# Two 16-head attentions: the divisor summed on VectorE before the weighting, the weights turned as one flat row, and more element-wise work on GpSimd

## The reference, cut to what matters

```python
# A: softmax with one more term in the divisor
attn = einsum('bhqd,bhkd->bhqk', qh * scale, kh)
e = exp(attn - max(attn))
attn = e / (1.0 + sum(e))
x = einsum('bhqk,bhkd->bhqd', attn, vh)      # then @ Wp.T + bp
# G: the same with a bias (16, 1024, 77) and a mask over the context rows
attn = where(mask, -inf, einsum('bhqd,bhkd->bhqk', q, k) * scale + bias)
probs = where(mask, 0.0, softmax(attn))
ctx = einsum('bhqk,bhkd->bhqd', probs / max(probs.sum(), 1e-6), v)   # then @ o_w.T + o_b
```

## Time and profile before

| | |
|---|---|
| median of 3 executions | 1403.33 us |
| the profiled execution | 1398.52 us, span 1396.5 us, mean granted clock 0.886 |
| busy, share of the span | PE 80%, PEld 60%, DVE 59%, ACT 42%, POOL 23% |
| layer A: first `shift` to last statistics | 24.2 to 166.1 us |
| layer G: first `shift` to last statistics | 955.4 to 1101.2 us |

### The profile page before, as it was taken

One profiled execution on the slowest core, in us unless ns is written; L12 is line 12 of the kernel. 1 busy time (PEld: TensorE's weight loads), 2 busy tenths in 40 slices (PEclk: granted clock), 3 DMA queues, 4 the chain that ended last, 5 costly groups with the idle time before them and its releaser, 6 DMA issues.

```text
span 1396.5 us, 22604 instructions
## 1 busy us (share of the span) xinstructions
PE 1121.6 (80%) x8519; PEld 844.9 (60%) x8519; DVE 819.8 (59%) x2107; ACT 580.9 (42%) x1448; POOL 314.9 (23%) x283
## 2 busy tenths in 40 slices
PE   4998799986989897957998899997888752996730
PEld 3666588884447545734666788884666731785530
DVE  5899722248558467972636764556888450552463
ACT  2665433342448535712415313225898440342210
POOL 0009134200435103420010000000000036435266
PEclk9899899995899899988999999997999655898775
DMA  9300054400000003000000720001221023444253
GB/s 316 129 2 2 19 160 131 125 1 0 1 0 2 1 1 121 2 12 12 1 23 2 202 90 1 0 1 37 74 74 38 24 84 105 135 136 115 92 152 118
DMA packets 59841, 88.74 MB, mean 64 GB/s; under 512 B 21315, under 2 KB 50749, under 8 KB 56925
## 3 DMA queue, kind: packets, MB, share of 16 engines
q1 hardware_dynamic: 52301, 67.05, 14.8%
q0 software_dynamic: 7440, 20.33, 5.3%
HBM read 60.60 MB, written 26.76 MB: 63 GB/s over the span
## 4 chain that ended last, share of the span: by engine, by line
PE 52%; DVE 19%; issue 11%; ACT 8%; POOL 4%; another core or an unknown queue 4%; DMA 1%; SPq 0%; POOLq 0%; DVEq 0%; ACTq 0%
PE ps L2571 5%; PE ps L1405 4%; PE ps L1939 4%; PE ps L800 4%; PE ps L813 4%; ACT work L487 2%; POOL pack_F L2830 2%; PE ps L2585 2%; PE ps L1950 2%; PE ps L380 2%; DVE dpack L1731 1%; PE ps L366 1%; DVE work L628 1%; ACT work L494 1%
## 5 line engine op out<-in xcount | busy, mean ns | idle before, releaser
L2822 POOL DMA_INDIRECT hall<-hall_rows,tile_idx x47 | 44.7, 950 | 381.0 <-DVE tile_idx L2728 328.2
L2571 PE MATMUL ps<-big,work 128*128 x316 | 89.2, 408 | 24.9 <-ACT work L2629 16.3
L1905 POOL TENSOR_TENSOR work<-work 128x512 f32<-128x512 f32 x64 | 65.1, 1039 | 143.6 <-DVE work L1753 143.6
L380 PE MATMUL ps<-work,hall 78*32 78x128 f32 (+1 forms) x2048 | 71.7, 282 | 17.4 <-ACT work L494 15.9
L2732 DVE TENSOR_TENSOR work<-work,ps 128x128 f32<-128x128 f32 x79 | 22.9, 290 | 106.4 <-ACT work L2633 51.0
L366 PE MATMUL ps<-pack_const,work 128*78 128x128 f32 (+1 forms) x512 | 73.8, 290 | 9.1 <-DVEq L593 9.1
L2571 PEld LDWEIGHTS ps<-big,work 128*128 128x128 f32 x316 | 58.1, 205 | 32.6 <-issue 27.4
L380 PEld LDWEIGHTS ps<-work,hall 78*32 78x32 f32 (+1 forms) x2048 | 53.9, 112 | 38.5 <-ACT work L494 33.2
L628 DVE RECIPROCAL work<-ps 128x128 f32<-128x128 f32 x64 | 60.8, 950 | 24.8 <-PE ps L380 24.8
L1855 ACT ACTIVATE work<-ps,work 128x256 f32<-128x256 f32 x128 | 58.9, 476 | 38.0 <-DVE work L1748 37.9
L487 ACT ACTIVATE work<-work 128x77 f32<-128x77 f32 x256 | 67.3, 347 | 14.3 <-DVE work L615 13.5
(11 more groups left out here) (515 smaller groups left out, 2644.9 us busy)
## 6 DMA issues: line engine op xcount, KB each, us to landing
expert_rows<-work SPq DMA_DIRECT2D x39, 256.0 KB
masked_bias<-hall SPq DMA_DIRECT2D x8, 1232.0 KB, 5.2
dpack<-masked_bias SPq DMA_DIRECT2D x8, 1232.0 KB, 6.2
hall<-in_fside SPq DMA_DIRECT2D x8, 616.0 KB, 7.4
dpack<-in_pack_D SPq DMA_DIRECT2D x1, 4115.0 KB, 15.7
big<-in_w SPq DMA_DIRECT2D x4, 1024.0 KB, 11.9
big<-in_pack_B SPq DMA_DIRECT2D x1, 2052.0 KB, 10.3
pack_F<-in_pack_F SPq DMA_DIRECT2D x1, 2052.0 KB, 22.4
```

What stands on the lines that cost most here:

```text
L380: mm = nc.tensor.matmul(ps[j * HB32:(j + 1) * HB32, 4, half:half + P], lhsT, A["pT"][0:SK[L], u % 2, h * P:(h + 1) * P], start=g == 0, sto ...
L2571: mm = nc.tensor.matmul(ps[:, GU_B[j % 2], 0:2 * INTER], MW["xT"][:, j % 2, c * P:(c + 1) * P], big[:, bass.ds(at + c * 2 * INTER, 2 * INT ...
```

## The change

Both attentions are rewritten on all four compute engines.

- The counting products are gone. DVE sums the exponentials of a unit (`tensor_reduce` of 128x624 in A, 128x616 in G), takes the reciprocal of 128x8 sums (`weigh_sum`), and POOL multiplies the exponentials by it, over 128x624 or 128x616 (`share`), before they are turned. `normalise` goes; ACT copies the 128x128 result out of PSUM instead (`take_o`).
- The weights of a unit are turned as one flat row of 8 x 78 or 8 x 77 columns, in five transposes of up to 128 columns; ACT copies 128x640. The values are laid out to match (`vflat`): with one-hot shifts of `vs` by 16 small matmuls at the start of a layer (`spread_values`), after which a unit needs 8 matmuls.
- In G the maximum is subtracted by POOL (`below_max`, 128x616), and ACT takes one exponential of 128x616.
- The projection's bias times its gate is added to x by POOL ahead of time (`gated_bias`, `add_bias`, 128x256), so `update` on DVE is two instructions.
- The loop runs over 16 groups `g` (one tile, two units) with three groups in flight.
- The rounding of B's weights moves from one run of twelve 128x2048 passes to pieces of 128x512, three and two passes each, placed on POOL between the shares of groups 9 to 16; the two all-reduces and scales stand behind the shares of group 6. `ffn_max_dve` is in groups 4 and 5.

Semaphores of other layers are renamed to make room; their order is the same.

```diff
+            def turn_p(k, xs):
+                pe.wait_ge(s("pn_ready"), k + 1 + done(L, "pn_ready"))
...
+                for r in range(NCHUNK):
+                    n = chunk_rows(L, r)
+                    mm = nc.tensor.transpose(ps[0:n, PT_BANK + r // 4, r % 4 * P:(r % 4 + 1) * P],
+                                             flat_weights(L, k)[:, r * P:r * P + n], ident)
...
+            def weigh_v(k):
+                m = k % (B * DC)
+                pe.wait_ge(s("pT_ready"), k + 1 + done(L, "pT_ready"))
...
+                for e in range(2):
+                    for j in range(HPG):
+                        r, g = VBLOCKS[2 * j + e]
+                        n = chunk_rows(L, r)
+                        mm = nc.tensor.matmul(ps[g * HB32:(g + 1) * HB32, 4, 0:P], KV["vflat"][0:n, 2 * j + e, m, :],
+                                              A["pT"][0:n, k % 2, r * P:(r + 1) * P], start=e == 0, stop=e == 1,
...
+            for g in range(NG16 + 2):            # PE
+                n, co = g // 2 + 1, g % 2
+                if n < HT:
+                    queries(n, co)
+                if g >= 2:
+                    weigh_v(2 * (g - 2) + 1)
+                if 1 <= g <= NG16:
+                    turn_p(2 * (g - 1), min(2 + g // 2, HT))
...
+                if g >= 2:
+                    project(g - 2)
+                if g % 2 and n + 1 < HT:
+                    turn_x(n + 1)
...
+                if 1 <= g <= NG16:
+                    weigh_v(2 * (g - 1))
+                if g + 1 < NG16:
+                    scores(g + 1)
...
+                if 1 <= g <= NG16:
+                    turn_p(2 * (g - 1) + 1, min(2 + (g + 1) // 2, HT))
...
                 else:
-                    for h in range(HPC):
-                        e = nc.scalar.activation(p[:, h, :], sub[:, h, :], ACT.Exp, bias=A["mx"][:, u % 2, h:h + 1])
-                    e.then_inc(s("p_ready"), 1)
+                    act.wait_ge(s("below_ready"), k + 1)
+                    nc.scalar.activation(p, sub, ACT.Exp).then_inc(s("p_ready"), 1)
...
+            for g in range(NG16 + 2):            # ACT
...
+                if 1 <= g <= NG16:
+                    exps(2 * (g - 1) + 1)
+                if n < HT:
+                    take_q(n, co)
...
+                if g >= 2:
+                    take_o(2 * (g - 2) + 1)
+                if 1 <= g <= NG16:
+                    take_pT(2 * (g - 1))
...
+                if g < NG16:
+                    exps(2 * g)
+                if 1 <= g <= NG16:
+                    take_o(2 * (g - 1))
...
+                if 1 <= g <= NG16:
+                    take_pT(2 * (g - 1) + 1)
...
+            gated_bias()                         # POOL
+            for g in range(NG16 + 1):
+                if g:
+                    share(2 * (g - 1))
+                if L == "A" and g >= QUANT_AT:
+                    ffn_round_pool(pool, g - QUANT_AT)
+                if L == "G" and g < NG16:
+                    below_max(2 * g)
+                if g:
+                    share(2 * (g - 1) + 1)
+                if L == "A" and g == QUANT_AT - 3:
+                    ffn_scale_pool(pool)
+                if L == "A" and g >= QUANT_AT:
+                    ffn_error_pool(pool, g - QUANT_AT)
+                if L == "G" and g < NG16:
+                    below_max(2 * g + 1)
+                if g < NG16:
+                    add_bias(g)
...
+            for g in range(NG16 + 2):            # DVE
+                if g < NG16:
+                    shift(g, 0)
...
+                if 1 <= g <= NG16:
+                    weigh_sum(2 * (g - 1) + 1)
...
+                if g < NG16:
+                    shift(g, 1)
...
+                if g >= 2:
+                    update(g - 2)
+                if g < NG16:
+                    weigh_sum(2 * g)
...
+        QUANT_AT = 9
+        QCOLS = 512
...
+            link(gp.tensor_scalar(q, w, inv, MAGIC, ALU.mult, ALU.add))
+            link(gp.tensor_scalar(q, q, -MAGIC, 127.0, ALU.add, ALU.min))
+            link(gp.tensor_scalar(q, q, -128.0, scale, ALU.max, ALU.mult))
...
+            chain_pool.link(gp.tensor_tensor(q, q, w, ALU.subtract))
+            gp.tensor_tensor(w, w, q, ALU.add).then_inc(sem("B_quantised"), 1)
```

More of the change, by code:

```diff
@@ L324, in turn_x @@
                 mm.then_inc(s("xT_ps"), 1)
-            def queries(n, parts=range(DC)):
-                if parts[0] == 0:
-                    pe.wait_ge(s("xT_ready"), nth(n, 1, 0) + done(L, "xT_ready"))
-                    if n >= 2:
-                        pe.wait_ge(s("x_new"), nth(n - 2, B, 0) + done(L, "x_new"))
-                for co in parts:
-                    for ci in range(DC):
-                        mm = nc.tensor.matmul(ps[:, Q_BANK, co * D:(co + 1) * D],
-                                              w["wq"][:, ci * D + co * P:ci * D + (co + 1) * P],
-                                              A["xnT"][:, ci, :], start=ci == 0, stop=ci == DC - 1)
-                if parts[-1] == DC - 1:
-                    mm.then_inc(s("q_ps"), 1)
@@ L349, in scores @@
+            def scores(g):
+                n, b = divmod(g, B)
+                if b == 0:
+                    pe.wait_ge(s("q_ready"), nth(n, 2, 1) + done(L, "q_ready"))
+                if g < 2:
+                    pe.wait_ge(s("kv_ready"), (2, 5)[g] + done(L, "kv_ready"))
+                if g:
+                    pe.wait_ge(s("sub_ready"), 2 * g + done(L, "sub_ready"))
+                for c in range(DC):
+                    at = c * HPT * SC
                     for j in range(S_TILES):
@@ L385, in project @@
-            def project(i, b, parts=range(DC)):
-                for c in parts:
-                    if c == 0:
-                        pe.wait_ge(s("on_ready"), nth(i, NU, 2 * b + 1) + done(L, "on_ready"))
-                        if b == 1:
-                            pe.wait_ge(s("q_ready"), min(i + 3, HT) + done(L, "q_ready"))
-                        if i or b:
-                            pe.wait_ge(s("x_new"), nth(i, B, b - 1) + done(L, "x_new"))
+                mm.then_inc(s("s_ps"), 1)
@@ L402, in heads16_pe @@
             turn_x(0)
[L403 removed]
+            queries(0, 0)
+            queries(0, 1)
             if L == "A":
                 values_ctx()
[L406 to L423 removed]
+            turn_x(1)
@@ L497, in heads16_act @@
[L497 to L517 removed]
+                    act.wait_ge(s("em_ready"), 2 * k + 1)
@@ new lines, in take_values, with take_spread @@
+                v = ve.tensor_tensor(vs, ps[0:SC, CTXV_BANK, :].rearrange("p (b n) -> p b n", b=B), bv, ALU.add)
+                if L == "G":
+                    for b in range(B):
+                        link(v)
+                        v = ve.tensor_scalar(vs[:, b, :], vs[:, b, :], keep[:, b:b + 1], None, ALU.mult)
+                v.then_inc(s("kv_ready"), 1)
+            def take_spread(part):
+                dve.wait_ge(s("kv_ps"), 3 + part + done(L, "kv_ps"))
+                half = KV["vflat"][:, part * NVB // 2:(part + 1) * NVB // 2].rearrange("p k m e -> p (k m e)")
+                ve.tensor_copy(half, ps[:, (CTXV_BANK, CTXK_BANK)[part], :]).then_inc(s("kv_ready"), 1)
@@ L638, in heads16_dve @@
             normed(1)
-            shift(0, 0)
+            take_values()
             spread_k(2)
             spread_k(3)
-            spread_v()
-            for n in range(HT):
-                shift(n, 1)
-                if L == "A" and n == 0:
+            for g in range(NG16 + 2):
+                if g < NG16:
+                    shift(g, 0)
+                if g == 0:
+                    take_spread(0)
+                    take_spread(1)
+                if 1 <= g <= NG16:
+                    weigh_sum(2 * (g - 1) + 1)
+                if L == "A" and g == 1:
+                    norm_std_dve(dve, "A1", REST)
+                    below(REST)
+                    dve.wait_ge(s("xT_ps"), 2 + done(L, "xT_ps"))
+                    normed(2)
+                    dve.wait_ge(sem("gates_ready"), 1)
+                if g < NG16:
+                    shift(g, 1)
+                if L == "A" and g == 0:
@@ L660, in heads16_dve @@
+                if L == "A" and g == QUANT_AT - 1:
                     ffn_inv_dve(dve)
[L661 to L674 removed]
```

425 lines of the change are left out of this document (200 added, 225 removed), and 12 rows, old and new, of the table TOTALS.

## The result

The changed kernel took 1407.0 us (median of 20 runs, 1398.5 to 1413.7), the kernel before 1396.1 us on the same chip (20 runs): ratio 1.0077, 95% interval 1.0059 to 1.0095. It is slower by 0.8%, where 1385 us and a gain were forecast. The profiled execution spans 1403.6 us, 7.1 more than that of before.

A forecast was written before the change was run, and what follows sets the result against it. DVE was taken as fullest in both layers, 6.3 us a group, with POOL pacing A's groups 9 to 15. G's -32.5 and A's +15 made -17.5 from 1403.3: 1386, stated as 1385 us, range 1366 to 1406.

The forecast's parts named there:

- three passes of 128x512: Rounding on POOL in layer A's groups 9 to 15: 0.65 us a pass, 1.9 us for the three.
- Groups 9 to 15: Layer A: POOL, not DVE, sets the pace at 7.5 us a group, 52.5 us for seven.
- The tail: End of layer A from group 16: share, rounding, share, then turn, copies, product, projection and update, 9 us.
- The all-reduces: Layer A, group 6: four POOL configuration changes, 2 x 6.7 + 2 x 6.9 = 27.2 us, giving 25.4 us of stop.
- the upper end: Change to an all-reduce costs between 0 and 6.7 us on POOL; 6.7 was taken.
- Rival 1: Layer A: changing to the all-reduce is free, stop 12.1 us instead of 25.4, kernel 1372 us; chance 0.17.
- Groups 2 to 8 with maxima and stop: Layer A: seven groups at 6.3 us (44.1), two maxima on DVE (4.6), all-reduce stop (25.4).
- -31.7 and -0.8: Layer G ends 31.7 us sooner; dropped zero-filling on DVE shortens layer F's end by 0.8 us.
- lower bound of 6.05: Steady group in A and G: DVE's summed work of 6.05 us with no wait at all.
- Rival 4, the clock: PE falls to half clock and stays, becoming the bound: 1438 us if everywhere; chance 0.11 for 1407 and above.
- Old order: Layer A: DVE's update no longer stopped by POOL's products, one operand now from PSUM; gain inside the sum.
- -32.5 against +15: Layer G gives back 32.5 us, layer A costs 15 us, together -17.5 us.

The follow-up runs named there:

- e1_same_kind: Changed kernel with its three rounding passes on POOL re-paired, arithmetic apart from min and max: 1381.9 us, 0.9881 of the kernel before.
- v3_again: Changed kernel with same-kind pairs, third pass writing the rounded weights, error products gone, maximum over partitions by TensorE and DVE: 1338.3 us, 0.9597 of the kernel before.
- e3_no_rounding: Changed kernel without all-reduces, rounding passes and error products, layer B's weights unrounded: 1341.0 us, 0.9584 of the kernel before.
- m1_prices: Changed kernel with a list of linked POOL instructions, 128x512 and 128x2048, ahead of layer A; one execution, read for durations only.
- b1_before_mixed: Kernel before with its rounding in the changed kernel's three mixed passes, each on 128x2048: 1405.4 us, 1.0064 of the kernel before.

## Why the prediction was wrong

The step that failed is the price of "three passes of 128x512 (0.18 fixed and a quarter of 1.9 each, 0.65: 1.9)" in the groups 9 to 15 of A. It took one price for all TENSOR_SCALAR passes from the earlier trace rows, where L745 pairs plus with times, while two of the three new passes pair plus with min and max with times. The kernel before had kept these apart, in four passes of 0.93 ns a column. Measured: 0.69 + 1.93 + 2.00 = 4.62. With that, the group took 10.66 us instead of 7.5, and POOL kept the bound that the forecast had rightly given it, at a much higher price; pairing the operations otherwise (e1_same_kind) gave back 21.6 us of A. That kernel takes 0.9881 of the kernel before, 16.6 us less on the scale of 1396, where 17.5 were forecast for the change: this one price decided the sign, and what else was off came near to cancelling out.

How the rest came out, by its own terms:
- **Groups 9 to 15**: 10.66 us instead of 7.5, 22 us for seven. Of the 3.16 us, 2.7 are the passes; the products (1.27 instead of 1.04) add 0.5, because their price was taken from L1905, which has one operand broadcast as a share has, while they read two whole tiles; the bias (0.72 instead of 0.46) adds 0.3; shares and gaps were cheaper. From group 9 to A's end the forecast had 61.5 us; there were 88.4 (DVE's first reduction of group 9 is at 117.88). This 26.9 is more than the whole miss of 24.6 (+7.1 by the profiled executions, against -17.5). The tail has 4.8 of it, 2.7 of them by the same passes in group 16.
- **The all-reduces**: the choice of the upper end was right. 26.12 us against 25.4, with 5.50, 7.38, 5.84 and 7.09 for what was taken as 6.7 and 6.9. Rival 1 falls. The rule of the Trainium skill (GPSIMD Engine Reference, section 2.1, Instruction dispatch), some 6 us for the first call to a freshly loaded kernel, agrees in size with all four gaps, 5.5 and 5.8 in one direction and 7.1 and 7.4 in the other, and the gap came at every change, not once.
- **Groups 2 to 8 with maxima and stop**: forecast 74.1, measured 74.5 (43.42 to 117.88). That is luck in part, since two errors cancel in it: the plain group took 5.73 us instead of 6.3 (DVE's shift 50.10, then 55.83), while the group with the stop took 0.65 more than its forecast and the one behind it 7.83 (110.05 to 117.88, with 1.1 us of other DVE work among it).
- **G**: -34.5 against -31.7 and -0.8. Its groups took 5.8 instead of 6.3, below even the lower bound of 6.05. The pass that reads PSUM (L685) took 0.75 and the sum (L701) 0.78 where 0.80 was taken, so that the durations of a group add up to 5.95; and many instructions are recorded as starting 0.08 to 0.09 us before the one ahead of them has ended, so that the steady group takes 5.71. Durations of rows, added up, are thus no lower bound of DVE's time. Its two ends cost 5 us more than written: groups 0 and 1 14.3 instead of 11.8, the tail 15.5 instead of 13.
- **Rival 4, the clock**: didn't happen, but its premise didn't come about either. PE's group was put at 4.5 us of 6.3, 71%; measured, the plain group of A from 50.10 to 55.83 has PE busy for 5.36 of 5.73 us, and the fourteen groups of G 5.28 of 5.82, over 90%. With 0.5 each, queries and projection were priced at half of what they took (1.03). The granted clock stood at 1.00 there, and at 1.00 from 50 to 80 us, where TensorE had 23.8 of 30 us (79%). In the second half of A the clock fell (0.74) while TensorE waited for POOL, and it was back at 1.00 in v3_again, where that wait was gone. A smaller fall needs no POOL: in e3_no_rounding it was 0.83 from 70 to 80 us, behind two waits of 1.6 and 1.3 us for DVE. The Trainium skill (TensorE: Matmul & The Clock Gate, Part 4, PE-mode transpose), weighed for this rival, is neither confirmed nor refuted: five transposes a unit were among the work at 1.00, but in no run do steady groups leave PE idle as much as the prediction had it.
- **Old order**: that the new update from PSUM would not be stopped by POOL was right: L609 stayed at 0.48 us in A beside a POOL that is 96% busy.

The forecast's sign hung on -32.5 against +15; the second number was 40. Its base was 7 us high besides: the three executions shown ahead of it had a median of 1403.3, twenty have 1396.1, so that 1385 stood for less of a gain than was worked out. No rival had a POOL whose own passes are dearer than the row they were priced by, though the diff showed the operations paired anew.

## What to carry to other kernels

Price a pass by its operations, not by its opcode: an instruction that the trace has only with one pair of operations has no price for another, and where the engine is to become the fullest, the unknown belongs in the range as a rival. On POOL keep minimum and maximum together and arithmetic apart, put instructions that need one configuration behind each other, and take whatever is needed once, such as a maximum over partitions, to an engine that need not change its configuration. Fewer passes are no gain by themselves: three took 4.62 us where four of the old kind would take about 2.6, an estimate from m1_prices (0.61 to 0.69 each). And a busy POOL is not free even off the critical path: in b1_before_mixed the longer passes slowed DVE's updates with two operands in SBUF.

## What the runs showed of the hardware that was not expected

- On POOL, f32, 128 partitions: times-plus, plus-times and min-max take 0.61 to 0.69 us for 512 columns and 1.9 to 2.1 for 2048; plus-min and max-times take 1.92 to 2.02 and 7.1 to 7.2.
- A change between all-reduce and ordinary instructions costs 5.5 to 6.1 us on the way to the all-reduce and 6.9 to 7.8 on the way back, each time, inside one program (all runs that have both).
- A DVE update with two operands in SBUF waits for POOL. In b1_before_mixed the one at 144.57 ended at 148.92, 0.28 us behind the product that ran from 144.13 to 148.64. Beside the slow passes it was let through earlier: three of them ended 2.31 us before the pass did (the one at 131.29 at 134.46, in a pass that ran to 136.77). The Trainium skill (SBUF — State Buffer, section SBUF: two separate sides) describes a pair of ports which DVE needs for two SBUF inputs, and says that the loser is blocked for the whole instruction. The products agree with it; the slow passes do not; what POOL does in their last 2.31 us was not tried. Beside the fast passes of the kernel before, too, an update ended 0.28 us behind the pass (108.06 + 1.34, in L746 that ended at 109.12). The same update with one operand from PSUM (L609) was never longer than 0.485 us in A and G of the kernel after.
